# A four-layer decoder on one core: layer 2's feed-forward in three steps per unit of attention, a feed-forward's low parts moved to GpSimd

## The reference, cut to what matters

```
x = x + _L0_xattn_ref(_layernorm(x), ctx, ...);  x = x + _L0_ffn_ref(_layernorm(x), ...)
x = x + _L1_xattn_ref(_layernorm(x), ctx, ...);  x = x + _L1_ffn_ref(_layernorm(x), ...)   # ffn: MXFP4 of rows and weight
x = x + _L2_xattn_ref(_layernorm(x), ctx, ...);  x = x + _L2_ffn_ref(_layernorm(x), ...)   # ffn: 16 of 64 rank-16 adapters
x = x + _L3_xattn_ref(_layernorm(x), ctx, ...);  x = x + _L3_ffn_ref(_layernorm(x), ...)
```

```
def _L1_ffn_ref(x, weight, bias):      # per block of 32: scale 2^(floor(log2(amax)) - 2), E2M1 values
    return jnp.einsum('bsk,nk->bsn', quantize_mxfp4(x), quantize_mxfp4(weight)) + bias
def _L2_xattn_ref(query, key, value, Wq, Wk, Wv, Wo):   # 32 heads of 16 over 8 key heads, softmax, Wo
def _L2_ffn_ref(x, A, B, Wr):          # scores = x @ Wr.T; gates = softmax(top 16); (x A) * gates @ B * 2
```

## Time and profile before

| | |
|---|---|
| median of 3 runs | 1607.87 us (1606.40 to 1609.18) |
| profiled execution | 1607.15 us |
| its span, first to last instruction | 1605.4 us |
| TensorE busy | 1534.7 us, 96% |
| DVE, ScalarE, GpSimd busy | 836.7, 762.0, 519.2 us |
| mean granted TensorE clock | 0.990 |

### The profile page before, as it was taken

The page is one execution under the profiler, slowest core; times in us unless marked ns, Lnnn a source line. Parts: engine busy times, 40 slices in busy tenths (PEclk is TensorE's granted clock), DMA queues, the critical chain, the costliest instruction groups (busy, mean ns, idle before and its releaser), DMA issues. The chain is left out here.

```text
span 1605.4 us, 26173 instructions
## 1 busy us (share of the span) xinstructions
PE 1534.7 (96%) x9596; PEld 1279.3 (80%) x9602; DVE 836.7 (52%) x1719; ACT 762.0 (47%) x2551; POOL 519.2 (32%) x648
## 2 busy tenths in 40 slices
PE   8999998899999999999999998878999999999998
PEld 6877887788989888888888897655666687888876
DVE  4666777454344555454444437677566421343465
ACT  4555454445455455445454564445444312455552
POOL 7667772322222222222221223334222000124324
PEclk9999999999999999999999999989999999999999
DMA  8000001011010101001010110001010001123101
GB/s 249 9 8 8 8 2 41 27 60 40 27 40 27 40 27 40 27 1 40 27 40 27 40 53 1 0 30 53 1 40 1 4 27 49 35 77 82 47 26 63
DMA packets 44415, 58.06 MB, mean 36 GB/s; under 512 B 25472, under 2 KB 32656, under 8 KB 41472
## 3 DMA queue, kind: packets, MB, share of 16 engines
q1 hardware_dynamic: 43872, 56.05, 11.2%
q10 hardware_dynamic: 352, 0.34, 0.1%
q0 software_dynamic: 64, 0.00, 0.0%
HBM read 48.77 MB, written 2.10 MB: 32 GB/s over the span
## 5 line engine op out<-in xcount | busy, mean ns | idle before, releaser
L1844 ACT ACTIVATE big<-pb 128x128 f32<-128x128 f32 x384 | 106.5, 277 | 306.8 <-PE pb L883 199.1
L2214 POOL TENSOR_TENSOR big<-big 128x512 f32<-128x512 f32 x96 | 100.0, 1042 | 257.4 <-DVE big L1476 257.4
L1893 ACT ACTIVATE big<-pb,big 128x128 f32<-128x128 f32 x384 | 135.8, 367 | 63.4 <-issue 40.2
L1471 DVE TENSOR_REDUCE big<-pb 128x4 f32<-128x512 f32 x96 | 65.9, 686 | 182.3 <-PE pb L922 174.7
L898 PE MATMUL pb<-wkh,CXh 128*128 128x256 f32 x512 | 149.9, 293 | 0.0
L2204 POOL TENSOR_SCALAR big<-big 128x6 f32<-128x6 f32 x64 | 12.9, 201 | 417.7 <-ACT big L1844 417.4
L898 PE MATMUL pb<-wkl,CXh 128*128 128x256 f32 x512 | 145.2, 283 | 0.0
L898 PE MATMUL pb<-wkh,CXl 128*128 128x256 f32 x512 | 144.3, 282 | 0.0
L1261 DVE TENSOR_TENSOR X<-X,pb 128x512 f32<-128x512 f32 x128 | 86.8, 678 | 76.2 <-PE pb L1109 39.2
L949 PE MATMUL pb<-woh,oh 128*128 128x512 f32 x256 | 111.9, 437 | 5.4 <-DVE X L1261 5.0
L883 PE MATMUL pb<-wqh,CXh 128*128 128x512 f32 x256 | 101.9, 398 | 4.5 <-DVE big L1441 3.1
(11 more groups left out here) (284 smaller groups left out, 3998.9 us busy)
## 6 DMA issues: line engine op xcount, KB each, us to landing
big<-in_w SPq DMA_DIRECT2D x17, 1024.0 KB, 5.0
big<-in_w SPq DMA_DIRECT2D x24, 256.0 KB, 3.0
big<-in_w SPq DMA_DIRECT2D x8, 512.0 KB, 3.6
o<-o SPq DMA_DIRECT2D x96, 32.0 KB, 1.9
X<-in_x SPq DMA_DIRECT2D x8, 256.0 KB, 4.9
big<-in_cn SPq DMA_DIRECT2D x8, 256.0 KB, 2.7
CXlf<-in_cT SPq DMA_DIRECT2D x8, 256.0 KB, 4.9
big<-in_wa SPq DMA_DIRECT2D x1, 2048.0 KB, 8.1
```

What stands on the lines that cost most here:

```text
L1471: v.tensor_reduce(m[j % 2], quarters(bank(p)), AX, MAX, negate=True).then_inc(S.m, 1)
L1844: y = a.activation(sq[i % 2], bank(p)[:, j * width:j * width + 128], ACT.Square, accum_out=ss[i % 2][:, first + j:first + j + 1])
L1893: y = a.activation(e_[:, c], bank(p)[:, c], ACT.Exp, bias=m[j % 2][:, k:k + 1], scale=1.0, accum_out=z[j % 2][:, k:k + 1])
L2214: g.tensor_tensor(quarters(e_), quarters(e_), bc(r[j % 2], 128), MUL).then_inc(*on.to(S.pn))
```

## The change

The ffn's pipeline is started at every third step instead of every second, and gets three steps in a unit: ahead of `l1_k` (place 3), ahead of `l1_d` (place 8) and behind it (place 9), from step 59 on. The blank stage stays, and `f1_quant` is no longer drawn to the front of its step. After the attention it gets three steps per step too, the first four queries standing between them. `l2_q` is then spread one per step, each one step sooner. The banks of three stages follow: `f1_mm` of the first six tiles takes bank 5 (was 7, which it shared with `l1_d`), and `f1_turn` and `l2_turn` keep their banks 3 and 2 for one and two tiles longer. `f2_split`'s subtraction moves from DVE's program to GpSimd's, at the same place of `ORDER`.

By unit the new `ORDER` reads (61 as an example): `l1_q61 l1_b60 l1_t59 f1_turn0 f1_norm1 l1_k61 l1_s60 l1_n61 l1_z60 l1_v59 f1_mm0 f1_quant1 l1_d58 l2_stats0 f1_stats2`. Before, unit 61 read: `l1_q61 l1_b60 l1_t59 f1_quant0 f1_stats1 l1_k61 l1_s60 l1_n61 f1_norm1 l1_z60 l1_v59 l1_d58`.

```diff
--- before.py
+++ after.py
@@ -99,8 +99,7 @@
 
     def queries_at(u):
 
-        return {1: [2, 3], 2: [4], 3: [5], 4: [6], 5: [7], 6: [8], 7: [9], 8: [10], 9: [11], 10: [12, 13],
-                12: [14, 15]}.get(u)
+        return [u + 3] if 1 <= u < 13 else None
 
 
     l0 = [("l0_mask", 2), ("l0_rows", 1), ("l0_out", 7), ("l0_sum", 4), ("l0_ctx", 7), ("l0_weigh", 6), ("l0_turn", 5),
@@ -112,7 +111,7 @@
     l1 = [("l1_q", 0), ("l1_b", 1), ("l1_t", 2), ("l1_k", 0), ("l1_s", 1), ("l1_n", 0), ("l1_z", 1), ("l1_v", 2),
           ("l1_d", 3)]
     f1 = ["f1_stats", "f1_norm", "f1_quant", "f1_wait", "f1_turn", "f1_mm", "l2_stats", "l2_rows", "l2_turn"]
-    ffn1 = pipeline([2 * t for t in range(NT)], [(s, None if s == "f1_wait" else every) for s in f1], ("f1_quant",))
+    ffn1 = pipeline([3 * t for t in range(NT)], [(s, None if s == "f1_wait" else every) for s in f1])
 
     l2_kv = pipeline(range(4), [("l2_kv", every)])
     pipe2 = batch_steps(16, [("f2_rows", 7, odd), ("l3_rows", 12, odd), ("f2_o", 11, odd),
@@ -158,23 +157,22 @@
         together(next(att1), (ffn0, 3), (ffn0, 6), (ffn0, 9))
     order.append(("f1_begin", 0))
     for step, stages in enumerate(att1, 7):
-        if step < 60:
+
+        sides = {64: [(l2_kv, 0)], 65: [(l2_kv, 0), (l2_kv, 9)], 66: [(l2_kv, 0)]}.get(step, [])
+        if step < 59:
             together(stages)
-        elif step < 64:
-            together(stages, (ffn1, 3), (ffn1, 6))
-        elif step == 64:
-            together(stages, (l2_kv, 0), (ffn1, 3), (ffn1, 6))
-        elif step == 65:
-            together(stages, (l2_kv, 0), (ffn1, 3), (ffn1, 6), (l2_kv, 9))
+        elif step == 59:
+            together(stages, (ffn1, 9))
         else:
-            together(stages, (ffn1, 0), (l2_kv, 0), (ffn1, 9))
+            together(stages, *sides, (ffn1, 3), (ffn1, 8), (ffn1, 9))
     order.append(("l2_begin", 0))
     for step in range(16 + 6):
         for name, i in next(pipe2):
             if name == "ffn1":
-                if step == 1:
-                    order.extend(("l2_q", j) for j in range(2))
-                run(1, ffn1)
+                for k in range(3):
+                    run(1, ffn1)
+                    if step == 0 and k < 2:
+                        order.extend([("l2_q", 2 * k), ("l2_q", 2 * k + 1)])
             elif name == "l2_q":
                 order.extend((name, j) for j in i)
             else:
@@ -258,11 +256,11 @@
         return ([("w4", (3,))] if weight_turn(i) is not None else []) + [("p", (7,))]
     sh = (0, 5, 6, 7)
     if stage == "f1_turn":
-        return [("p", (3,) if i < 5 else sh)]
+        return [("p", (3,) if i < 6 else sh)]
     if stage == "f1_mm":
-        return [("p", (7,) if i < 5 else sh)]
+        return [("p", (5,) if i < 6 else sh)]
     if stage == "l2_turn":
-        return [("p", (2,) if i < 3 else sh)]
+        return [("p", (2,) if i < 5 else sh)]
     if stage == "f3_turn":
         return [("p", (0,))]
     if stage == "f3_mm":
@@ -1595,11 +1593,6 @@
                 on.mark(v.tensor_scalar(g_, g_, nm_[:, 1:2], 2.0, MUL, MUL))
                 marks.gates[t] = on.n
 
-            def f2_split(j):
-                x, hi, lo = f2_parts(j)
-                on.wait_ge(S.f2h, j + 1)
-                v.tensor_tensor(lo, x, hi.bitcast(F32), SUB).then_inc(S.f2l, 1)
-
             def f2_h(t):
                 on.wait_ge(S.dve, marks.gates[t])
                 if t:
@@ -1670,7 +1663,7 @@
                       l0_out=l0_out, f0_split=f0_split, f0_quant=f0_quant, f0_quant_u=f0_quant_u, f0_gate=f0_gate,
                       f0_silu=f0_silu, f0_quant2=f0_quant2, f0_down=f0_down, l1_begin=l1_begin, l1_keys=l1_keys, l1_k=l1_k, l1_n=l1_n,
                       l1_b=l1_b, l1_s=l1_s, l1_z=l1_z, l1_v=l1_v, l1_d=l1_d, f1_quant=f1_quant,
-                      f1_mm=f1_mm, l2_a=l2_a, l2_s=l2_s, l2_z=l2_z, l2_v=l2_v, l2_c=l2_c, f2_split=f2_split, f2_a=f2_a, f2_h=f2_h,
+                      f1_mm=f1_mm, l2_a=l2_a, l2_s=l2_s, l2_z=l2_z, l2_v=l2_v, l2_c=l2_c, f2_a=f2_a, f2_h=f2_h,
                       f2_o=f2_o, l3_begin=l3_begin, l3_keys=l3_keys, l3_values=l3_values, l3_main=l3_main, l3_q=l3_q, l3_a=l3_a, l3_z=l3_z, l3_v=l3_v, l3_c=l3_c, f3_mm=f3_mm)
             for stage, i in ORDER:
                 if stage in do:
@@ -2246,6 +2239,12 @@
                     on.wait_ge(S.r2, n + 1)
                     on.wait_ge(*on.last)
                     g.tensor_tensor(s3, s3, bc(r2[n % 2], 64), MUL).then_inc(*on.to(S.p2))
+
+            def f2_split(j):
+                x, hi, lo = f2_parts(j)
+                on.wait_ge(S.f2h, j + 1)
+                on.wait_ge(*on.last)
+                g.tensor_tensor(lo, x, hi.bitcast(F32), SUB).then_inc(*on.to(S.f2l))
 
             def l3_z(i):
                 probs(64 + i, E3[i % 2], r3)
```

More of the change, by code:

```diff
@@ L2286, in pool_program @@
             do = dict(begin=begin, l0_bias=l0_bias, l0_norm=l0_norm, l0_mask=l0_mask, l0_sum=l0_sum, l0_ctx=l0_ctx, f0_norm=f0_norm,
-                      f0_silu=f0_silu, f0_down=f0_down, l1_k=l1_k, l1_z=l1_z, f1_quant=f1_quant, l2_begin=l2_begin, l2_a=l2_a, l2_z=l2_z,
+                      f0_silu=f0_silu, f0_down=f0_down, l1_k=l1_k, l1_z=l1_z, f1_quant=f1_quant, l2_begin=l2_begin, l2_a=l2_a, l2_z=l2_z, f2_split=f2_split,
                       l3_z=l3_z, l3_c=l3_c, f3_mm=f3_mm)
```

## The result

| | before | after |
|---|---|---|
| median | 1607.86 us | 1616.91 us (1616.07 to 1617.38) |
| ratio, 95% interval | | 1.0053 [1.0041, 1.0065] |
| profiled execution, its span | 1607.15, 1605.4 | 1617.38, 1615.6 |

What follows compares the result with a forecast made beforehand. TensorE, 96% busy, bounds the kernel; its waits, restarts and lower clock lose 39.1 us. Waits of 24.3 + 5.9 + 7.35 = 37.5 give -1.6, the clock +5.4: span 1609.2, with 1.75 outside it 1611 us; range 1601 to 1618.

Steps and rivals of the forecast that it cites:

- the forecast's own 1608 to 1615: Whole kernel: range of the case that the forecast itself holds, chance 0.44, around 1611 us.
- The waits of the units: Units 61 on, layer 2's ffn beside attention: TensorE waits for DVE's quantised rows and turns of rows, sum 24.3 us.
- F' = F+15.4: From one quantisation's end (F), when f1_turn can start, to the next one's end: 15.4 us, against 12.55 of TensorE's work.
- The clock: Edited area: seven longer gaps or pairs make TensorE's clock fall more often; 5.4 us not covered, bounds 0 and 15.
- rival one: No clock loss on the path: all falls land in waiting time, 1605.6 us, chance 0.22.
- The low parts on GpSimd: Layer 3's attention steps: 5.5 us leave DVE, 10.2 go to GpSimd, steps take 6.0, TensorE waits 7.35 us.
- low parts that find GpSimd idle: Attention's steps: one of the signs named that would show the forecast wrong; no size given.
- the account of the queries: New phase: queries read two steps after their product, so ScalarE's evacuation, a 1.9 us wait, is awaited no more.
- the same steps lost 17: Attention's steps before the edit: they lost about 17 us with their clock, set against 7.35 us of new waits.
- GpSimd holds DVE: Rival, chance 0.10: half of the low parts' 10.2 us on GpSimd and a unit's slip come through, 1618 us.
- The attention's start runs free: Rival, chance 0.24: GpSimd's low parts delay nothing, the 7.35 us of waits vanish, 1603.6 us.
- Everything before 958 is untouched: The part of the kernel before 958 us, ahead of the edit: claimed untouched, with no term for it.

Runs made afterwards that it cites:

- after_repeat: The changed kernel run once more, unaltered, in a later set of four runs: 1613.87 us, ratio 1.0045 to the kernel before.

## Why the prediction was nearly right, point by point

The forecast of 1611 lay at the edge of what can't be told from before, with chances of 0.40 for the same and 0.36 for slower; slower it was. In part that was luck. The 1616.91 us lie outside the forecast's own 1608 to 1615 and nearest to the 1618 of a rival whose cause is refuted below; the repeat's 1613.87 lie inside. What the mechanism can answer for is the stretch, and there +3.8 us stood against +4.7.

**The waits of the units: right, a little too large.** It gave F' = F+15.4 and units of 14.15, 15.4, 15.4 and 13.6; the rows of L737 show 16.7, 15.2, 15.4 and 13.4. The first is longer by a fall of the clock (978.2 to 985.0), and the last, forecast at 13.6, is no sign of a faster chain. `f1_turn` waits for DVE 14.4 us in six times, the first 3.75 (forecast: 15 to 18, six or seven, 4); the turn of rows waits 6.8 (forecast 9). In unit 62 the squares started 1.4 us behind `l1_k`'s end (forecast 1.5 to 2):

```profile
998.50 0.81 ACT L1701 ACTIVATE xn<-X,ve,rs 128x512 f32<-128x512 f32 x1 [2.17 <-POOL ve L2102]
...
1000.64 0.26 ACT L1837 ACTIVATE big<-pb 128x128 f32<-128x128 f32 x1
```

L1292 took 1.35, 1.04, 1.15, 1.04 and 0.75 us in quant(0) to quant(4), the last one under the 1 us named. `f2_a(0)` came later, at 1133.2.

**The clock: two terms that can't be told apart.** Seven gaps were named and five falls came. The waits, with the gaps' 0.17 each, came out 5.1 us under the forecast (32.4 against 37.5), and the clock's part at 10.1 us of capacity against 5.4 forecast on the path. A slow matmul fills a wait, so one term's excess is in part the other's shortfall; only their sum was forecast to a microsecond (42.9, measured 42.5, and that is partly luck). Set against the corrected 38.6 of before, the forecast would have been half a microsecond higher, +4.3 for the stretch where the profiles show +4.7 and +4.4. How much of a fall reaches the end is shown in one case: in after_repeat the third fall lasted 3.4 us instead of 6.8, the turn of rows waited 1.1 us longer (7.9), and the stretch was only 0.3 shorter. That fall was nearly all covered, as rival one says. Its time, 1605.6, didn't come all the same.

**The low parts on GpSimd: the step's length right, the attribution wrong.** The 7.35 us of waits in the attention's steps came out at 3.4 + 2.6 = 6.0. But 2.4 of them, the waits of 1.35 and 1.08 us for ScalarE's exponentials at 1090 and 1095, end before GpSimd's first low part starts (1095.74), and before the edit the same two kinds of wait came to 5.7 and 3.6:

```profile
PE pb L1029 <- ACT big L1975: 3.6, 3, 1.5
```

So at most 3.6 us can be the low parts' doing. One named sign of being wrong, low parts that find GpSimd idle, showed for the first pair alone: 3.1 us of GpSimd's idle time lie before it, spent waiting for ScalarE's high part. And the text valued the part itself at nothing but these costs. The 5.6 us of idle time before L1601, which stands in the earlier trace rows, was not used: TensorE's waits behind it went to the account of the queries and of "the same steps lost 17". This step failed as an account: the part wins 7.1 us alone and 11.0 here. A reader of the prediction would have dropped the part that helps most.

**The rivals.** "GpSimd holds DVE" is refuted for the low parts of this kernel (L1537 at 692 ns beside eight GpSimd operations of 1.27 us; it reads one operand from PSUM, so it isn't the case of two SBUF inputs that the rule weighed speaks of), and shown for the bias addition, with 3.6 us of the stretch. The Trainium skill, SBUF — State Buffer, "SBUF: two separate sides", has VectorE and GpSimd take their shared port pair for a whole instruction: the bitwise operation agrees (1.35 us beside an addition of 1.28, 0.42 without). No run here has the low parts beside such an operation. "The attention's start runs free" did not happen: 6.0 us of its waits stayed, and GpSimd was full from 1098 to 1116. But its direction was nearer the truth than the forecast's, since the low parts' move by itself makes the kernel faster (1600.97).

**"Everything before 958 is untouched": true of the instructions, false of the time.** This is the term that was missing. Of the profiled execution's 6.4 us above the forecast (1617.38 against 1610.95) 5.9 were lost there, 0.9 in the stretch, and 0.4 came back behind it. Less what was lost ahead, both profiled spans of the changed kernel (1615.6 - 5.9 and 1611.3 - 1.6) are 1609.7 us, where 1609.2 was forecast. Why an execution's clock falls more often in layer 1 is open. Whether the change makes it likelier is open too: four executions in one set took 1616 to 1617 us, four in the other 1613 to 1614, and no run separates that. Before itself ranged from 1605.1 to 1611.6 us over some 60 executions and never reached the 1613 that a loss of 5.9 would give, so the suspicion stands.

## What to carry to other kernels

An instruction that waits for another engine costs what stands behind it in its queue: its idle time in the groups by line (here 5.6 us before eight operations of 0.69) is the first thing to price when it is moved, and moving it one step later on its own engine did as much here as moving it to another engine (tried in the old order only). Three steps of a chain in one unit left next to no slack between them here, and when one distance was lengthened the next constraint took over most of the wait, so a change of order is best tried one stage and one bank at a time. And a median is only as good as the part of the program that the edit doesn't touch: compare the times between two fixed instructions in both traces.

## What the runs showed of the hardware

In layer 1's stage (90 to 335 us, TensorE busy 91%) the same instructions took 5.9 us more in one profiled execution than in another, at a granted clock of 0.95 for 0.97 over the window; over 14 profiles the shift ran from -0.5 to 6.7 us and grew with the time at the lower clock, 6.8 to 27.3 us. A bitwise operation of 128x512 int32 on DVE took 0.75 to 1.35 us instead of 0.42 when it ran beside GpSimd's fp32 addition of the same size, and ended 0.28 us behind it, while DVE's additions out of PSUM (692 ns) kept their time beside GpSimd's subtractions.
